# One expert tile fewer, an earlier read of the gate values, and another order of the last additions in an attention and expert kernel

## The reference

```python
xn = _layernorm(x)
scores = einsum('btd,de->bte', xn, router_w)
routing_weights, routing_idx = top_k(softmax(scores), 2)      # divided by their sum
gate = einsum('bted,edf->btef', dispatched, gate_proj)        # f = 352
up   = einsum('bted,edf->btef', dispatched, up_proj)
expert_out = einsum('btef,efd->bted', silu(gate) * up, down_proj)
out = x + attention(xn) + einsum('bted,bte->btd', expert_out, expert_w)
```

## Time and profile before

| | |
|---|---|
| Timed runs, median of 3 | 1246.61 us (1245.76 to 1248.01) |
| Profiled execution, its own time | 1249.39 us |
| Span of the profiled execution | 1247.6 us |
| Busy in the span: PE / DVE / ACT / POOL | 93% / 72% / 58% / 26% |
| Chain that ended last: PE / DVE / issue / DMA / POOL | 81% / 8% / 3% / 3% / 3% |

### The profile page before, as it was taken

One profiled execution on the slowest core, in us unless ns is written; L12 is line 12 of the kernel. 1 busy time (PEld: TensorE's weight loads), 2 busy tenths in 40 slices (PEclk: granted clock), 3 DMA queues, 4 the chain that ended last, 5 costly groups with the idle time before them and its releaser, 6 DMA issues.

```text
span 1247.6 us, 58621 instructions
## 1 busy us (share of the span) xinstructions
PE 1162.6 (93%) x24462; PEld 1037.9 (83%) x24463; DVE 900.1 (72%) x2518; ACT 718.6 (58%) x1707; POOL 325.4 (26%) x461
## 2 busy tenths in 40 slices
PE   6899999999999999999999999998979999999990
PEld 5688888878887888888788878887869999999980
DVE  6888778877887887788788778877873444444446
ACT  5666566646765565656476566746544555555550
POOL 4000111111111111111111111231572555555550
PEclk9999999999999999999999999999998999999995
DMA  7000000000000000000000000002245777777779
GB/s 244 1 4 6 12 12 12 14 12 12 15 12 11 15 14 12 12 15 13 12 14 15 12 12 15 14 25 59 72 115 191 263 273 263 272 262 267 268 258 378
DMA packets 59943, 109.40 MB, mean 88 GB/s; under 512 B 9072, under 2 KB 30192, under 8 KB 59728
## 3 DMA queue, kind: packets, MB, share of 16 engines
q1 hardware_dynamic: 49216, 82.80, 19.3%
q0 software_dynamic: 9216, 19.19, 4.7%
q10 hardware_dynamic: 1296, 4.19, 0.8%
HBM read 28.94 MB, written 24.58 MB: 43 GB/s over the span
## 4 chain that ended last, share of the span: by engine, by line
PE 81%; DVE 8%; issue 3%; DMA 3%; POOL 3%; ACT 1%; SPq 0%; POOLq 0%; DVEq 0%; ACTq 0%
PE bank L1250 12%; PE bank L1252 10%; PE bank L1251 10%; PE bank L1536 8%; PE bank L1424 8%; PE bank L1350 6%; PE bank L1402 5%; PE bank L1289 4%; PE bank L1387 4%; PE bank L1376 4%; PE bank L1336 3%; PE bank L1413 2%; DVE qs L850 2%; PE bank L1368 1%; PE bank L1516 1%
## 5 line engine op out<-in xcount | busy, mean ns | idle before, releaser
L1219 DVE TENSOR_TENSOR aT<-bank,aT 128x256 f32<-128x256 f32 (+1 forms) x216 | 91.4, 423 | 148.4 <-ACT aT L771 142.9
L505 POOL COPY xn<-meta 128x2 f32<-128x2 f32 x128 | 26.9, 210 | 655.6 <-PE bank L1387 292.4
L606 POOL DMA_INDIRECT expert_rows<-yt,wdi x144 | 140.2, 973 | 144.5 <-ACT yt L777 121.5
L644 ACT ACTIVATE kn<-bank 128x512 f32<-128x512 f32 x128 | 69.5, 595 | 145.3 <-PE bank L1336 145.2
L1250 PE MATMUL bank<-xTh,Wh 128*128 128x256 f32 x512 | 152.4, 298 | 0.6 <-DVE xs L844 0.6
L662 ACT ACTIVATE qs<-qs,cvec 128x128 f32<-128x128 f32 x480 | 146.1, 395 | 0.2 <-DVE cvec L899 0.2
L1251 PE MATMUL bank<-xTh,Wl 128*128 128x256 f32 x512 | 145.6, 284 | 0.0
L1252 PE MATMUL bank<-xTl,Wh 128*128 128x256 f32 x512 | 145.4, 284 | 0.0
L509 POOL DMA_INDIRECT sorted_tokens<-xn,slot x128 | 124.7, 974 | 52.1 <-POOL xn L505 49.6
L1250 PEld LDWEIGHTS bank<-xTh,Wh 128*128 128x128 f32 x512 | 98.5, 192 | 47.8 <-issue 44.7
L1250 PE MATMUL bank<-xtTh,cw 128*128 128x256 f32 (+1 forms) x432 | 134.3, 311 | 2.1 <-issue 2.1
(11 more groups left out here) (216 smaller groups left out, 2687.2 us busy)
## 6 DMA issues: line engine op xcount, KB each, us to landing
cw<-guh SPq DMA_DIRECT2D x73, 352.0 KB
cw<-gul SPq DMA_DIRECT2D x73, 352.0 KB
xt<-sorted_tokens SPq DMA_DIRECT2D x73, 132.0 KB, 2.3
er<-expert_rows SPq DMA_DIRECT2D x15, 512.0 KB, 7.7
xa<-in_x SPq DMA_DIRECT2D x8, 512.0 KB, 10.9
out<-xa ACTq DMA_DIRECT2D x7, 512.0 KB, 8.2
gu<-in_gate_up_w SPq DMA_DIRECT2D x8, 352.0 KB, 3.3
expert_rows<-yt,wdi POOLq DMA_INDIRECT x144, 2.5
```

The source lines that it names most:

```text
L606: pool.indirect_dma_start(ys_d, bass.IndirectOffsetOnAxis(ap=wdi[:, q:q + 1], axis=0), yt[:, q, :], None).then_inc(f_sc[q], 16)
L1219: last = dve.tensor_tensor(a_, bank[1 + FT * s + t][0:k, W:2 * W], a_, ALU.mult)
```

## The change

Four things are altered.

1. `TILES` becomes 71. It is no longer a multiple of 4. Each engine runs 17 rounds of its loop and then a remainder of 3 tiles written out behind it. In the last of these no next tile is prepared (no rows turned over on PE, no copies of them on ACT and DVE, no load by SP).
2. SP's last loads go away with it: SP writes out two iterations behind its loop and so loads up to tile 70, where it loaded up to tile 72.
3. The four `gate` values are read before the tiles, behind `f_te`.
4. On DVE the lower additions are no longer done ahead of all upper ones. Batch 0's stands first. Then comes a wait for all scatters, and then, batch by batch, the lower addition directly ahead of the upper one.

```diff
-TILES = K2 * C // 2 + E
+TILES = K2 * C // 2 + E - 1
...
+        LOOPS, REST = TILES // RD, TILES % RD
+        def tiles_at(r):
+            return LOOPS + (1 if r < REST else 0)
...
             sp.wait_ge(f_te, 1)
+            done = [sp.value_load(gate[0:1, n:n + 1], min_val=16 * LANDED, max_val=16 * (LOOPS + 1 + LANDED)) for n in range(RD)]
...
+            with sp.Fori(0, LOOPS) as i4:
                 for r in range(RD):
-                    i = i4 * RD + r
-                    sp.wait_ge(f_yt, ev(2, i - RD + 1, 1))
-                    sp.sem_inc(s_pass, 1)
-                    load_tile(i + 1, (r + 1) % RD)
-                    load_weights(i + 1, (r + 1) % RD)
+                    load_next(i4, r)
+            for r in range(REST - 1):
+                load_next(LOOPS, r)
             for n in range(RD):
-                done = sp.value_load(gate[0:1, n:n + 1], min_val=16 * LANDED, max_val=16 * (TILES // RD + LANDED))
                 for h in range(2):
-                    sp.wait_ge(f_sc[2 * (RD - 1 - n) + h], done)
+                    sp.wait_ge(f_sc[2 * (RD - 1 - n) + h], done[n])
                     sp.sem_inc(s_pass, 1)
...
-            for b in range(B):
+            def add_lower(b):
                 dve.wait_ge(o_in0[b], 16)
                 xb = xa[:, b * CB:(b + 1) * CB, :]
                 dve.tensor_tensor(xb, xb, er0[b][:], ALU.add).then_inc(o_add, 1)
+
+            add_lower(0)
+            for r in range(RT):
+                dve.wait_ge(f_sc[r], 16 * (tiles_at(r // 2) + LANDED))
             for n, (b, lo, hi) in enumerate(PIECES):
+                if b > 0 and lo == 0:
+                    add_lower(b)
                 dve.wait_ge(o_in1[n], 16)
                 dve.wait_ge(o_add, b + 1)
                 xb = xa[:, b * CB + lo:b * CB + hi, :]
...
+            def tile_products(i4, r, ex1, last=False):
+                i, s = i4 * RD + r, r % 2
+                ex = tile_expert(r)
+                gate_up(i, r, s, 0, i4 + 1)
+                gate_up(i, r, s, 1, i4 + 1)
+                if not last:
+                    pe.wait_ge(f_xt[(r + 1) % RD], 16 * (i4 + 1) if r < RD - 1 else 16 * (i4 + 2))
+                    transpose_tile(i + 1, (r + 1) % RD)
+                gate_up(i, r, s, 2, i4 + 1)
+                if not last:
+                    load_expert(i + 1, r + 1)
+                if r == 0:
+                    pe.wait_ge(f_dn, 48)
+                down_(i - 1, 1 - s, ex1)
+                return ex
```

More of the change, by code:

```diff
@@ L435, in _, with load_next @@
             sp.wait_ge(f_ms, 2)
-            with sp.Fori(0, TILES // RD) as i4:
-                for r in range(RD):
-                    i = i4 * RD + r
-                    sp.wait_ge(f_yt, ev(2, i - RD + 1, 1))
-                    sp.sem_inc(s_pass, 1)
-                    load_tile(i + 1, (r + 1) % RD)
-                    load_weights(i + 1, (r + 1) % RD)
+            def load_next(i4, r):
+                i = i4 * RD + r
+                sp.wait_ge(f_yt, ev(2, i - RD + 1, 1))
+                sp.sem_inc(s_pass, 1)
+                load_tile(i + 1, (r + 1) % RD)
+                load_weights(i + 1, (r + 1) % RD)
+            with sp.Fori(0, LOOPS) as i4:
+                for r in range(RD):
+                    load_next(i4, r)
+            for r in range(REST - 1):
+                load_next(LOOPS, r)
             for n in range(RD):
-                done = sp.value_load(gate[0:1, n:n + 1], min_val=16 * LANDED, max_val=16 * (TILES // RD + LANDED))
                 for h in range(2):
-                    sp.wait_ge(f_sc[2 * (RD - 1 - n) + h], done)
+                    sp.wait_ge(f_sc[2 * (RD - 1 - n) + h], done[n])
                     sp.sem_inc(s_pass, 1)
@@ L454, in _ @@
             for r in range(RT):
-                sp.wait_ge(f_sc[r], 16 * (TILES // RD + LANDED))
+                sp.wait_ge(f_sc[r], 16 * (tiles_at(r // 2) + LANDED))
             for n, (b, lo, hi) in enumerate(PIECES):
@@ L596, in _, with rows_out @@
             pool.memset(aT[:, 1], 0.0).then_inc(f_ms, 1)
-            with pool.Fori(0, TILES // RD) as i4:
-                for r in range(RD):
[L599 to L607, removed]
+            def rows_out(i4, r):
+                i = i4 * RD + r
+                for h in range(2):
+                    q = 2 * r + h
+                    pool.wait_ge(f_sc[q], 16 * (i4 + LANDED))
+                    pool.wait_ge(f_wd, ev(1, i))
+                    pool.wait_ge(f_yt, ev(2, i, h))
+                    pool.sem_inc(s_pass, 1)
+                    pool.indirect_dma_start(ys_d, bass.IndirectOffsetOnAxis(ap=wdi[:, q:q + 1], axis=0),
+                                            yt[:, q, :], None).then_inc(f_sc[q], 16)
+            with pool.Fori(0, LOOPS) as i4:
+                for r in range(RD):
+                    rows_out(i4, r)
+            for r in range(REST):
+                rows_out(LOOPS, r)
             for r in range(RT):
-                pool.wait_ge(f_sc[r], 16 * (TILES // RD + LANDED))
+                pool.wait_ge(f_sc[r], 16 * (tiles_at(r // 2) + LANDED))
         @block.scalar
@@ L777, in result, with tile_out @@
                 act.activation(yt[:, q, :], bank[7][:, P * h:P * h + P], ACT.Copy, scale=xt[:, q, WGT:WGT + 1]).then_inc(f_yt, 1)
-            with act.Fori(0, TILES // RD) as i4:
-                for r in range(RD):
[L781 to L787, removed]
+            def tile_out(i4, r, last=False):
+                i, s = i4 * RD + r, r % 2
+                gate_out(i, s, 0)
+                gate_out(i, s, 1)
+                if not last:
+                    tile_hi(i + 1, 1 - s)
+                gate_out(i, s, 2)
+                for h in range(2):
+                    result(i - 1, (r - 1) % RD, h, i4 + (1 if r == 0 else 2))
+            with act.Fori(0, LOOPS) as i4:
+                for r in range(RD):
+                    tile_out(i4, r)
+            for r in range(REST):
+                tile_out(LOOPS, r, r == REST - 1)
             for h in range(2):
-                result(TILES - 1, RD - 1, h, TILES // RD + 1)
+                result(TILES - 1, REST - 1, h, LOOPS + LANDED)
             for n, (b, lo, hi) in enumerate(PIECES):
@@ L1223, in _, with tile_inner @@
             dve.wait_ge(f_ms, 2)
[L1224 to L1228, removed]
+            def tile_inner(i4, r, last=False):
+                i, s = i4 * RD + r, r % 2
+                inner(i, s, 0)
+                inner(i, s, 1)
+                if not last:
                     tile_lo(i + 1, 1 - s)
                     tile_meta(i + 1, (r + 1) % RD, i4 if r < RD - 1 else i4 + 1)
-                    inner(i, s, 2)
-            for b in range(B):
+                inner(i, s, 2)
+            with dve.Fori(0, LOOPS) as i4:
+                for r in range(RD):
+                    tile_inner(i4, r)
+            for r in range(REST):
+                tile_inner(LOOPS, r, r == REST - 1)
+            def add_lower(b):
                 dve.wait_ge(o_in0[b], 16)
@@ L1545, in _ @@
             pe.wait_ge(f_wl, E)
-            with pe.Fori(0, TILES // RD) as i4:
+            def tile_products(i4, r, ex1, last=False):
+                i, s = i4 * RD + r, r % 2
+                ex = tile_expert(r)
+                gate_up(i, r, s, 0, i4 + 1)
+                gate_up(i, r, s, 1, i4 + 1)
+                if not last:
+                    pe.wait_ge(f_xt[(r + 1) % RD], 16 * (i4 + 1) if r < RD - 1 else 16 * (i4 + 2))
+                    transpose_tile(i + 1, (r + 1) % RD)
+                gate_up(i, r, s, 2, i4 + 1)
+                if not last:
+                    load_expert(i + 1, r + 1)
[3 more added lines that the diff above has]
+                return ex
+            with pe.Fori(0, LOOPS) as i4:
                 ex1 = tile_expert(-1)
                 for r in range(RD):
[L1549 to L1561, removed]
+                    ex1 = tile_products(i4, r, ex1)
+            ex1 = tile_expert(-1)
+            for r in range(REST):
+                ex1 = tile_products(LOOPS, r, ex1, r == REST - 1)
+            down_(TILES - 1, (REST - 1) % 2, ex1)
 def laid_out(inputs):
```

## The result

| | median | range | against before |
|---|---|---|---|
| Before | 1246.99 us | 1245.76 to 1248.61 (5 runs) | |
| Changed kernel | 1240.33 us | 1238.19 to 1245.73 (5 runs) | 0.9958, 95% interval 0.9939 to 0.9977 |
| Changed kernel again, in the experiments | 1241.52 us | 1239.0 to 1247.22 (10 runs) | 0.9955, interval 0.9939 to 0.9970 |

A forecast was written before the change was run, and what follows sets the result against it. PE bounds the tiles, transfers the stretch after the last scatter's landing. 3.92 (tile, transposes) + 0.96 (stretch) - 0.08 (POOL busy) + 1.4 (landing) + 24.4 - 27.0 (tail) = 3.6 us saved: median 1243.0, range 1240.6 to 1246.3.

The forecast's parts named there:

- One tile and its transposes: On PE, one tile fewer takes 3.70 us off the path and the last tile's two transposes 0.22: 3.92 us.
- Code behind the loops: Rival, chance 0.07: PE pays 2.14 us at the loop's exit for the remainder of three tiles; end at 1245.1.
- The last scatter's issue: On POOL: last scatter issued at 1213.14 against 1217.94, 4.80 us earlier, of which 0.96 is the stretch that goes.
- Its landing: Last scatter lands 3.8 us after issue, bounds 2.2 and 6.4, half its life under the lower loads; before 5.15.
- The register loads ahead of the tiles: On SP before tile 0: four more register loads hidden by its wait for split weights, taken at nothing; uncovered, up to 3.8.
- The tail: From last landing to end, 27.0 us against 24.4: first upper load 3.6, DVE additions 19.1, last store 4.3.
- The sum: All terms together save 3.6 us: span 1247.6 to 1244.0, median 1246.61 to 1243.0.
- The range: Median between 1240.6 and 1246.3 us, said to hold four cases and leave out the delayed weights.
- all four cases: The forecast (0.68), slow scatters (0.12), code behind the loops (0.07) and hidden additions (0.06).
- the hidden additions: Rival, chance 0.06: the tail keeps its 24.4 us with additions hidden; 1241.4 in the span, 1240.4 as median.
- the scatters stay slow: Rival, chance 0.12: last scatter takes 6.4 us as under full load; 1.0 us saved, 1245.6 as median.
- Delayed weights: Rival, chance 0.07: lower loads delay tile 70's weights, PE stands 6.5 us; median put at 1250.

The follow-up runs named there:

- experiment 2: Only the 71 tiles against the kernel before, gate values read late and all lower additions first: 1243.38 us, 0.9967.
- Experiment 6: The changed kernel with the gate values read late, as before: 1244.51 us, 0.9958 against the kernel before.
- experiment 4: Only DVE's order of additions changed against the kernel before, 72 tiles and gate values read late: 1248.54 us, 1.0005.
- experiment 5: The changed kernel without DVE's new order, all lower additions first, gate values early: 1246.69 us against 1248.72 before, 0.9987.
- experiment 3: Only the gate values read early against the kernel before, 72 tiles and old order of additions: 1246.16 us, 0.9996.
- experiment 1: The changed kernel run again with no edit, for a second profile: 1241.52 us, 0.9955 against the kernel before.

## Why the prediction was right, and where its sizes were off

The direction, the places and their order were right. By the stretches the gain is 6.7 us where 3.6 were forecast, so two terms were off by more than a microsecond. Term by term:

- **One tile and its transposes, 3.92 us.** Measured 3.61 and 2.53, since PE waits once for a late transfer. Over all nine executions with 71 tiles it is 3.1 to 3.7 us, but for the one of 2.53. Without this wait the term was right: from the fifth results on, experiments 2 and 6 take 246.53 us both, 4.09 less than before. Of this, 0.18 is PE's wait for ACT ahead of the last down product (0.91 us in both, 1.09 before), which leaves 3.91.
- **Code behind the loops.** I had priced it at 2.14 us and given it 0.07, as an alternative to the forecast. It was there, as an addition to it, at 0.6 to 1.8 us. Its form was another one than I had thought of: not PE's own code missing, but a transfer landing late while a block of code was fetched. Experiment 6 differs from the changed kernel on SP alone and has its fetch elsewhere, so SP's code decides where it falls. That a long step goes where the fetch goes is shown by nine executions at three places. How the fetch makes a transfer late was not tried.
- **The last scatter's issue.** Forecast 2.51 us behind the last results, measured 2.55 (before 3.39). The stretched scatter is DVE's doing: experiment 4, with only DVE's order changed, has none and 2.43 us here, and experiment 5 shows the other side.
- **Its landing, 5.2 to 3.8 us.** Measured 2.65 and 2.45, up to SP's next issue. The lower loads ended where I had put them: the last lower piece, issued at 1207.06, landed 10.2 us later, 1.9 us behind the last scatter's issue at 1215.34 (forecast 2). What was mis-sized is what this costs. I took half a life under load as half of the extra time, but the scatter landed some 0.5 us behind the last lower piece, after 2.43 us. The twelve profiles agree: the landing took 2.23 to 2.24 us where the last lower piece landed at most 1.5 us behind the scatter's issue, 2.4 and 2.6 where it was 1.9 and 2.1, 4.8 to 5.8 where it was 4.6 to 6.2, and 5.2 and 6.1 where it was 8.5 and 9.9. What early lower loads are worth shows against experiment 6: 5.14 us with the loads 3.8 us later. The row of that last lower piece (the last number is the us to landing):

```profile
er<-expert_rows SPq DMA_DIRECT2D x1, 512.0 KB, 10.2
```

- **The register loads ahead of the tiles, at nothing.** Right: from SP's load before them to the first weights it is 8.33 and 7.74 us, against 8.07 before.
- **The tail, 27.0 us.** Measured 24.81. This was the step that was off most. The first landing was right (3.6; 3.45 on the chain). The additions took 18.6 instead of 19.1 us. An upper one was counted from 5.06 us for four, 1.265 each, while in the pair, 2.46 us a batch, they take 1.23. The last store was the largest miss: 2.57 instead of 4.3 us from the last addition's end. I had priced it near the store with others queued ahead of it (5.07); here its transfer landed after 2.1 us, since all upper loads had landed by 1235.7 and DVE's pairs spaced the stores out.
- **The sum.** By the stretches the gain was larger than forecast by 3.1 us: 2.2 from the tail and 1.2 from the landing, less 0.3 in the tiles. The timed ratio puts it at 1.6 (5.2 against 3.6), with an interval of 2.9 to 7.6 us that holds both. Only PE's wait worked against the other misses. So that the timed gain came nearer to the forecast than the stretches is no merit of the working.
- **The range.** 1240.6 to 1246.3 was said to hold all four cases, but the hidden additions (1240.4) and both ends of the forecast's own range (1240.4 and 1246.4) lie just outside it.

The rivals: "the scatters stay slow" does not hold for the changed kernel, but is what experiments 3, 4 and 6 show (5.1 to 6.1 us), so it was the right danger. "The additions stay hidden" fell: DVE is the chain. Still, the tail was only 0.4 us longer than before, since the transfers are nearly as long. "Delayed weights" by the lower loads fell: in the first profile of the changed kernel PE waited at tile 68, before the first lower load was issued (1202.80 against 1203.10), and not at tile 70. In the second profile the first lower load went out at 1197.59, 0.9 us before PE went on; there it may have added to the wait, and no run separates the two.

What each part is worth, by the sums of stretches against before (one profile each; the two of the changed kernel are 0.9 us apart):

| | tiles | gate | order | two parts | all |
|---|---|---|---|---|---|
| stretches, us | -4.4 | -1.2 | +1.9 | tiles and gate -0.7; tiles and order -3.7 | -6.7, -5.7 |
| timed ratio, us | -4.1 | -0.5 | +0.6 | tiles and gate -1.6; tiles and order -5.2 | -5.2, -5.6 |

Each timed value is known to about 2 us. The parts are not additive. The tile alone carries most of it. Early gate values without the order take most of the tile's gain back, and the timed ratios agree: 0.9987 against 0.9967 of the tiles alone, with intervals that overlap a little, and against 0.9955 of the changed kernel, with intervals that do not. That they pay once the order is there (2 to 3 us) is shown by the stretches only; the timed ratios do not tell the two kernels apart. The reason is that the first brings the lower loads in before the last scatter, and then eight additions are ready to run in a row and lock POOL out, unless the order keeps them back.

## What to carry to other kernels

When a transfer is brought forward, look at what it releases: here the eight additions that it made ready held POOL's scatter for 8 us, and the same earlier loads left 0.7 us of gain or about 6 by the stretches (1.6 or 5.2 to 5.6 timed), depending on an order of additions elsewhere. Count a tail twice, as a chain of one engine and as bytes over the bandwidth, since the longer of the two is the time: taking 3.7 us off the chain gave 1.3. And with runs that differ by 7 us in a stretch that computes the same, compare stretches of the traces between two marks and let the timed ratio confirm.

## What the runs showed of the hardware that was not expected

- A scatter on POOL does not always slip in between DVE additions. In experiment 5 it was held through all that were left of eight: 8.17 us instead of 0.97. There the additions began 1.13 us apart, each before the one ahead of it (1.21 us long) had ended. In experiment 2 the next addition began 0.12 us behind the end of the last, as its piece had just landed, and a scatter begun in the first one was through after 1.32 us, with a further addition behind it:

```profile
1207.24 1.23 DVE L1262 TENSOR_TENSOR xa<-xa,er 128x1024 f32<-128x1024 f32 x1 [0.41 <-DMA er<-expert_rows]
1208.59 1.23 DVE L1262 TENSOR_TENSOR xa<-xa,er 128x1024 f32<-128x1024 f32 x1
```

```profile
1207.98 1.32 POOL L615 DMA_INDIRECT expert_rows<-yt,wdi  x1 [0.30 <-issue]
```

  Every stretched scatter of this study ended 0.83 or 0.84 us behind the end of an addition: in experiment 2 that of 1207.24 + 1.23 = 1208.47 (scatter 1209.30), before that of 1216.79 (1217.63), in experiment 5 the last of the eight, 1214.55 (1215.39). A gap on DVE is not needed. In experiment 3 the next addition began 0.04 us before the last one ended, 1.18 us behind its start, and the scatter still got through, 0.84 us behind the first one's end:

```profile
1212.86 1.22 DVE L1235 TENSOR_TENSOR xa<-xa,er 128x1024 f32<-128x1024 f32 x1 [0.46 <-DMA er<-expert_rows]
1214.04 1.22 DVE L1235 TENSOR_TENSOR xa<-xa,er 128x1024 f32<-128x1024 f32 x1
```

```profile
1213.54 1.38 POOL L606 DMA_INDIRECT expert_rows<-yt,wdi  x1 [0.30 <-issue]
```

  So POOL was let in at starts 1.18 us apart and not at 1.13. What decides between the two is not shown.

  The Trainium skill (SBUF — State Buffer, "SBUF: two separate sides") speaks of a lock held for one instruction. That agrees with experiments 2 and 3. In experiment 5 it would have let the scatter go at the end of the addition that it met (1207.74), and the scatter would have been through 1.4 us after its start; the measurement decides against it there.
- A step of PE was longer by 0.6 to 1.8 us wherever one block of code (0.02 MB, one packet) was fetched among the tiles from 950 us on, beside transfers that landed late. The packet took 6.9% of the 16 engines' time in its microsecond in the changed kernel and 12.0% in experiment 1, where the step was the longest. A remainder of three tiles behind a loop was enough to bring it into the tiles.
- A store of 256 KB landed 2.1 us after its issue with one other of its size issued 0.6 us ahead of it and all loads done (first row, the changed kernel's last two), and 4.6 us behind a full queue (second row, the last one before):

```profile
out<-xa ACTq DMA_DIRECT2D x2, 256.0 KB, 2.1
out<-xa ACTq DMA_DIRECT2D x1, 256.0 KB, 4.6
```
